# A graph layer on one core: four weight products of an edge group in one row instead of two pairs

## The reference, cut to what matters

```python
h = relu(layernorm(x))
s, v = h[:, :64] @ W_nl0, einsum('nmi,mk->nki', h_vectors, W_nl1)
w = relu(edge_feature @ W_fc1) @ W_fc2          # 224 tensor-product weights per edge
w0, w1, w2, w3, w4 = split(w, [64, 128, 160, 192])
xs, xv = s[dst], v[dst]                          # rows gathered per edge
tp = concat(w0*xs, w3*dot(xv, r), (w1*xs) x r, w2*xv, w4*cross(xv, r))
agg = segment_sum(tp, src, N) / 32               # then W_out_s, W_out_v
out = x + gated(agg @ W_out + h @ W_skip)
```

## Time and profile before

| what | value |
|---|---|
| median of 3 runs | 1365.98 us |
| profiled execution, its own time | 1356.92 us |
| its span, first to last instruction | 1355.0 us |
| TensorE busy over the span | 1271.0 us (94%) |
| VectorE / ScalarE / GpSimd busy | 1207.4 / 1071.5 / 1080.8 us |
| mean granted TensorE clock | 0.984 of full speed |

### The profile page before, as it was taken

The page is one execution under the profiler, slowest core; times in us unless marked ns, Lnnn a source line. Parts: engine busy times, 40 slices in busy tenths (PEclk is TensorE's granted clock), DMA queues, the critical chain, the costliest instruction groups (busy, mean ns, idle before and its releaser), DMA issues.

```text
span 1355.0 us, 35147 instructions
## 1 busy us (share of the span) xinstructions
PE 1271.0 (94%) x9057; PEld 1142.1 (84%) x9057; DVE 1207.4 (89%) x4348; ACT 1071.5 (79%) x2574; POOL 1080.8 (80%) x1054
## 2 busy tenths in 40 slices
PE   3999979999999999977999999999999999999997
PEld 2777758888888888867899999999999999998996
DVE  6999988888889888856899999999999999999996
ACT  3999977888888888846788788878888888787785
POOL 6999988888878778417788888888888888888883
PEclk9999998999999999988999999999999999999999
DMA  3000003444434444325787887878777787878774
GB/s 109 1 0 0 0 23 83 109 111 113 108 104 118 109 113 108 91 71 140 215 241 227 231 230 230 239 225 240 227 233 228 232 231 233 238 229 234 227 233 128
DMA packets 90918, 212.25 MB, mean 157 GB/s; under 512 B 15030, under 2 KB 56281, under 8 KB 90878
## 3 DMA queue, kind: packets, MB, share of 16 engines
q1 hardware_dynamic: 62462, 155.23, 37.1%
q0 software_dynamic: 28416, 56.56, 17.6%
HBM read 127.73 MB, written 84.00 MB: 156 GB/s over the span
## 4 chain that ended last, share of the span: by engine, by line
PE 50%; POOL 18%; issue 13%; DMA 8%; ACT 5%; DVE 3%; ACTq 0%; POOLq 0%; SPq 0%; DVEq 0%
POOL mg L529 17%; PE bank L1042 7%; DMA mg<-messages,slot_m 7%; PE bank L1105 5%; PE bank L1049 5%; PE bank L1199 5%; PE bank L1184 4%; PE bank L1158 4%; PE bank L1134 3%; PE bank L1122 3%; PE bank L1089 3%; PE bank L1118 2%; PE bank L1120 2%; ACT nn L958 2%; PE bank L1176 2%
## 5 line engine op out<-in xcount | busy, mean ns | idle before, releaser
L529 POOL DMA_INDIRECT mg<-messages,slot_m x392 | 444.8, 1135 | 121.4 <-issue 110.2
L958 ACT ACTIVATE nn<-xb,n_bias,n_rstd 128x160 f32<-128x160 f32 x588 | 300.6, 655 | 22.3 <-DVE n_bias L628 21.4
L1199 PE MATMUL bank<-mg,hot 128*128 128x192 f32 x1568 | 299.2, 334 | 11.6 <-DVE hot L752 11.6
L1184 PE MATMUL bank<-wsk_a,nt_a 128*128 128x160 f32 x1568 | 294.8, 311 | 4.0 <-DVE ob L765 3.0
L1199 PEld LDWEIGHTS bank<-mg,hot 128*128 128x128 f32 x1568 | 251.7, 191 | 11.8 <-DVE hot L752 11.8
L480 POOL DMA_INDIRECT xg<-x,dst_g x200 | 207.4, 1037 | 61.9 <-issue 56.6
L1184 PEld LDWEIGHTS bank<-wsk_a,nt_a 128*128 128x128 f32 x1568 | 226.4, 192 | 13.2 <-issue 9.0
L610 DVE BATCH_NORM_STATS2 n_stat<-xb 128x6 f32<-128x160 f32 x784 | 186.6, 310 | 4.0 <-DMA xb<-x 3.8
L535 POOL TENSOR_TENSOR n_rstd<-n_sum,neg_half 128x8 f32<-128x8 f32 x98 | 163.7, 1671 | 15.4 <-DVE n_sum L624 13.4
L496 POOL TENSOR_SCALAR slot_r<-iota_slot,rank,row_no 125x128 bf16<-125x128 f16 x200 | 160.0, 804 | 6.1 <-DVE rank L659 0.5
L1176 PE MATMUL bank<-ident,nn 128*128 128x128 f32 x784 | 136.0, 296 | 26.1 <-ACT nn L958 21.9
(11 more groups left out here) (147 smaller groups left out, 2976.7 us busy)
## 6 DMA issues: line engine op xcount, KB each, us to landing
xb<-x SPq DMA_DIRECT2D x97, 640.0 KB, 6.0
out_dram<-ob SPq DMA_DIRECT2D x97, 640.0 KB, 3.6
messages<-msg SPq DMA_DIRECT2D x50, 390.6 KB
mg<-messages,slot_m POOLq DMA_INDIRECT x392, 5.2
ef<-edge_feat_t SPq DMA_DIRECT2D x50, 125.0 KB, 6.0
xg<-x,dst_g POOLq DMA_INDIRECT x200
xb<-x SPq DMA_DIRECT2D x1, 420.0 KB
out_dram<-ob SPq DMA_DIRECT2D x1, 420.0 KB
```

Source lines behind the costliest of these rows:

```text
L529: pool.indirect_dma_start(mg[:, u, k, :], None, messages[:, :], bass.IndirectOffsetOnAxis(ap=slot_m[:, u, k:k + 1], axis=0)).then_inc(n.g[ ...
L958: last = act.activation(nn[:, u % 2, h, :, g % 4], xb[:, u, g, :], ACT.Relu, bias=n_bias[:, u, g:g + 1], scale=n_rstd[:, u, g:g + 1])
L1184: pe.matmul(z[:, t, 0:F], nt_a[:, h, t * P:(t + 1) * P], wsk_a[:], start=(t % 2 == 0), stop=False, skip_group_check=True)
L1199: last = pe.matmul(q_z[h][:, t, 0:Z], hot[:, u % 2, g // 2, (g % 2) * P:(g % 2) * P + P], mg[:, u, g // 2, 0:Z], start=False, stop=True, s ...
```

## The change

All four weight products of a group are issued together, behind `project(0)`. The waits on `e_hid` and `e_wsb` and the increment of `e_w` are no longer tied to a particular tile.

```diff
                     def weights(tiles):
                         if not within(q):
                             return
-                        if 0 in tiles:
-                            pe.wait_ge(e_hid, q + 1)
-                            wait(pe, e_wsb, q)
+                        pe.wait_ge(e_hid, q + 1)
+                        wait(pe, e_wsb, q)
                         for t in tiles:
                             part = slice(EF * (t // 2), EF * (t // 2) + EF)
                             last = pe.matmul(p_w[:, t, :], hid[part, t % 2 * ET:(t % 2 + 1) * ET], wfc2[part, :],
                                              start=True, stop=True)
-                        if GE - 1 in tiles:
-                            last.then_inc(e_w, 1)
+                        last.then_inc(e_w, 1)
...
                     turn(1)
                     project(0)
-                    weights((0, 2))
+                    weights((0, 2, 1, 3))
                     turn(2)
                     project(1)
-                    weights((1, 3))
                     turn(3)
                     project(2)
```

## The result

The changed kernel takes 1374.13 us (median of 8 runs, 1372.89 to 1377.10); the kernel before, run beside it and counted with its first three runs, 1360.98 us (8 runs, 1359.80 to 1367.78). The ratio is 1.0103 (95% interval 1.0087 to 1.0118): 1.0% slower.

A forecast was written before the change was run, and what follows sets the result against it. The prediction took a closed loop through TensorE and ScalarE's message copy and normalisations to bound the steady rounds. 47 groups times 0.37 us gave 17.4 us, added to the median 1365.98 us: 1383.4 us, range 1377 to 1393.

The forecast's parts named there:

- The loop through put, the normalisations and `turn_rows`: Steady edge rounds: TensorE up to project(1), then 1.86 us through ScalarE to turn_rows, closes a loop of 7.75 us.
- The row holds TensorE 0.95 us and shifts the loop by 0.37 us: Ahead of turn(2): four products take 0.95 us where a pair took 0.58, so each round grows to 8.12 us.
- The Trainium skill's rule on weight loads: In the row: loads overlap matmuls only across differing row groups; dearer case 0.58 us a group, 1393.3 us; chance 8%.
- The row saves TensorE 0.30 us a group: TensorE's own work: one row of four costs 1.04 us against 1.34 us for two pairs.
- `turn(3)` waits 0.12 us and `project(2)` ends at 405.35: Behind project(1): turn(3) waits 0.12 us for take(2); project(2) ends before turn_rows at 406.11, so the wait costs nothing.
- What could absorb the shift: Other engines in a steady round: no reserve in the loop takes up the 0.37 us; GpSimd is at 78%.
- The term of the sum, 17.4 us: Edge stage, groups 2 to 48: 47 rounds, each longer by 0.37 us, add 17.4 us.
- The base: Time the shift was added to: 1365.98 us, the median of the runs, giving 1383.4 us.
- The prediction's other sum: Whole kernel: the profiled execution of 1356.92 us plus the shift would take 1374.3 us.
- Clock: Rival: TensorE's added idle time lowers its clock to 0.91 in the edge rounds, 29 us on top, 1412 us; chance 3%.
- absorption: Rival: ScalarE, idle 1.05 us a round, catches up the shift in the edge rounds; no change, 1366 us; chance 4%.
- TensorE bound: Rival: TensorE bounds the edge rounds after all, so each gains 0.18 us, 8.5 us in all, 1357.5 us; chance 4%.

The follow-up runs named there:

- n4_after: Changed kernel with ScalarE's four normalisations put together behind take(1): 1360.81 us, ratio 1.0011 to the kernel before.
- n4_before3: Kernel before with ScalarE's four normalisations put together behind take(1), third try, at the usual time: 1355.20 us, ratio 0.9972.
- row_0123: Changed kernel with its row of four products in tile order 0, 1, 2, 3 instead of 0, 2, 1, 3: 1375.43 us, ratio 1.0113.
- row_p1: Changed kernel with the row of four products moved from behind project(0) to behind project(1): 1343.46 us, ratio 0.9886 to the kernel before.
- g3: Both kernels with GpSimd gathering three of each group's four tiles: kernel before 1350.37 us (ratio 0.9930), changed kernel 1367.42 us (1.0062).
- a_again: Changed kernel, unaltered, profiled and timed again: 1373.75 us, ratio 1.0110 to the kernel before.
- b_again: Kernel before, unaltered, profiled and timed again: 1358.6 us, ratio 0.9996.
- eg_before3: Kernel before with the gathers of group 2 moved ahead of the table stage, third try, at the usual time: 1358.63 us, ratio 0.9999.
- eg_before: Kernel before with the gathers of group 2 moved ahead of the table stage, first try, where the unchanged kernel took 1444.29 us: 1447.03 us.

## Why the prediction was right in kind and wrong in size

- *The loop through put, the normalisations and `turn_rows` bounds the round.* Right, and tested: out of the loop (n4_after against n4_before3) the row's cost falls from 14 to 5.6 us.
- *The row holds TensorE 0.95 us and shifts the loop by 0.37 us.* Right to 0.01 us (0.96; rounds 7.72 and 7.80 became 8.09 and 8.17). The reason given, that the two halves of the array run side by side, was wrong (row_0123).
- *The Trainium skill's rule on weight loads ("TensorE: Matmul & The Clock Gate", "The mechanism")* was taken to give 0.58 us a group. The row inside a steady round shows four further passes at 0.37. There neighbouring products use different halves, so the sharper test is row_0123, where they share one: its products start 0.29, 0.19 and 0.19 us apart, as in the other order. The measurement decides against the rule here.
- *The row saves TensorE 0.30 us a group.* Right; in row_p1 it is the larger part of a gain of 16 us.
- *`turn(3)` waits 0.12 us and `project(2)` ends at 405.35 in the old round's time.* Half right. `turn(3)` starts 3.57 us after h (forecast 404.37 - 400.82 = 3.55). But `project(2)` waits in addition for the message copy, and starts at 430.02 - 425.71 = 4.31, not at about 3.9. It did no harm beside the longer loop, yet it is the bound in n4_after.
- *What could absorb the shift: nothing ("GpSimd is at 78%").* This is one of the two steps that failed. It looked for idle time in one steady round and in the mean, and so missed a round that comes once: round 4, in which VectorE waits 2.61 us for late rows. In the kernel before this costs 3.6 us and 0.35 in the next round, in the changed one 1.2, because its longer rounds leave TensorE less to wait and the clock did not fall. The term of the sum, 17.4 us, is 13 to 16 in the timed runs, and 17 with the long round 4 gone (g3). Why the rows land late, and why the clock falls at a stop of 0.94 us in row_0123 and not at one of 0.93 in a_again, stays open.
- *The base.* The other step, and the larger. The shift was added to 1365.98 us, the median of three runs. With five more runs that median is 1360.98. Of the 9.3 us between forecast and result 5.0 are this and 4.2 the shift. The range allowed 2 us for the spread of the runs; the three runs were one sample of a median that moved by 5. On the base of eight runs the forecast would have been 1378.4 us and the same range 1372 to 1388, with the result inside it. The prediction's other sum, 1356.92 + 17.4 = 1374.3 us, is 0.2 us from the result by luck: that one execution lacked the wait in round 4.
- *Clock, absorption, TensorE bound.* None came in the changed kernel's steady rounds: granted clock 1.00, ScalarE's idle time before hid unchanged, rounds longer and not shorter. But the lower clock came in the kernel before, in round 4 of b_again, where the forecast did not look. The rival was put low because the level changed at no short stop; in row_0123 it fell at one of 0.94 us.

## What to carry to other kernels

When independent work is moved within a round, ask which side of the closed loop it leaves and which it joins: the same row cost 14 us ahead of a projection that ScalarE waits for, and gained 16 us behind it, where it runs beside ScalarE's work. An engine at 99.7% on paper can still be the one that waits; compare starts with the releaser's end in two successive rounds. And list the length of every round, in more than one profile: a steady round and a mean share both hide a round that is long once, and a change that lengthens the others can shorten that one. An absolute forecast also needs a base of more than three runs.

## What the runs showed of the hardware that was not expected

- *Pairs of passes.* By the order of issue, the two fp32 passes of a product of 64 rows start together, in the order 0, 1, 2, 3 as in 0, 2, 1, 3 (row_0123: 404.97 and 404.98), and each product after the second takes 0.19 us for 224 columns. With 128 rows the passes follow one another: the two of L1122, 64 columns each, start at 426.90 and 427.01. Why is open.
- *A short stop and the clock.* In b_again the granted clock is at the lower level from 239.1 to 242.5 us, after TensorE stopped for 2.08 us; in row_0123 from 237.4 to 240.8, at a stop of 0.94. The same lowering near round 4 stands in eg_before3, n4_after, n4_before3 and row_p1, and in no profile of the usual regime with a round 4 of under 9.4 us.
- *Another regime.* Where the unchanged kernel took 1445 us, ScalarE starts instructions late whose operands TensorE seems to have finished. One round of eg_before there:

```profile
404.97 0.90 ACT L949 ACTIVATE w_sb<-bank 125x896 f32<-125x896 f32 x1
407.28 0.59 ACT L930 ACTIVATE ht<-bank 128x500 f32<-128x500 f32 x1 [1.41 <-remote]
407.76 0.27 ACT L931 ACTIVATE hz<-bank 128x125 f32<-128x125 f32 x1
408.78 0.54 ACT L925 ACTIVATE msg<-bank 125x448 f32<-125x448 f32 x1 [0.75 <-remote]
```

```profile
405.39 0.27 PE L1090 MATMUL bank<-ident,hn 125*128 125x125 f32 x1
```

  The copy ht needs `turn_rows`, whose last transpose started at 405.39, and starts at 407.28. The semaphore events in the trace say where the time is lost: the one that this transpose raises moves at 407.25, 1.59 us after the transpose's modelled end, and ht starts 0.03 us later. From 240 to 560 us the median of this delay is 1.59 us in eg_before (33 rounds) and 0.01 us in b_again (41 rounds). So ScalarE is not slow to start: the transposes end later than modelled, or their signal comes late. In 320 us the idle time comes to 38.0 us before ht and 15.4 before the message copy; most rounds take 8.6 to 10.3 us, some 12 to 13, and the granted clock is 0.95 over the stretch. The medians of the kernels there lay within 0.6% of each other, and the changed kernel with earlier gathers was the lowest both times. What makes the signals late, and whether the change by itself helps there, was not found; the 1.0% holds for the usual regime.
- *The opening.* In the first profile round 1 took 8.49 us with its row of four at 1.86 us; in b_again, eg_before3 and both profiles of the changed kernel it took about 7.0 us, with the row at 1.02 or 1.03. Every one of them has a stretch at the lower clock at the start of the edge stage; it lasts 17 us in the first profile (198.1 to 215.2) and 7 to 10 in the others.
